# A decoder layer on one core: the groups of work of a pipelined step written in another order on four engines

## What is computed

```
x = x + attn(layernorm(x))      # gated slot attention, 4 heads, 64 slots: a recurrence over time
x = x + xattn(layernorm(x), ctx) # cross attention, 16 heads, 64 keys of ctx, bias from positions, mask
x = x + ffn(layernorm(x))       # mixture of experts: top 2 of 8, capacity 1280, silu(x W1) * (x W3) W2
```

## Time and profile before

| what | value |
| --- | --- |
| median of 3 runs | 1478.4 us (1473.18 to 1479.07) |
| the profiled execution | 1473.74 us, its span 1472.0 us |
| PE matmuls busy | 1366.1 us, 93% of the span |
| PE weight loads busy | 1212.5 us, 82% |
| DVE busy | 949.4 us, 64% |
| ACT busy | 632.6 us, 43% |
| POOL busy | 343.2 us, 23% |
| mean granted TensorE clock | 0.969 of full speed |

### The profile page before, as it was taken

One profiled execution on the slowest core, in us unless ns is written; L12 is line 12 of the kernel. 1 busy time (PEld: TensorE's weight loads), 2 busy tenths in 40 slices (PEclk: granted clock), 3 DMA queues, 4 the chain that ended last, 5 costly groups with the idle time before them and its releaser, 6 DMA issues. The chain is left out here.

```text
span 1472.0 us, 32584 instructions
## 1 busy us (share of the span) xinstructions
PE 1366.1 (93%) x10841; PEld 1212.5 (82%) x10841; DVE 949.4 (64%) x3162; ACT 632.6 (43%) x1596; POOL 343.2 (23%) x524
## 2 busy tenths in 40 slices
PE   7799999999999999999848999999999999999995
PEld 5577777777777777777638999999999999999995
DVE  4578888887877887887654546555564645555442
ACT  2345445544544554544324434443443434444331
POOL 3112222322322322232220222211221112121122
PEclk9799999999999999999858999999999999999998
DMA  2731131101101100110003242321424142241111
GB/s 90 219 99 32 25 109 32 32 17 32 32 17 32 32 21 29 32 32 14 23 29 115 36 120 34 110 36 30 127 31 120 30 115 33 63 94 30 30 23 22
DMA packets 67319, 80.13 MB, mean 54 GB/s; under 512 B 11090, under 2 KB 60723, under 8 KB 67154
## 3 DMA queue, kind: packets, MB, share of 16 engines
q1 hardware_dynamic: 52562, 59.09, 13.1%
q0 software_dynamic: 14592, 18.91, 7.7%
HBM read 44.04 MB, written 33.96 MB: 53 GB/s over the span
## 5 line engine op out<-in xcount | busy, mean ns | idle before, releaser
L856 ACT ACTIVATE h_a<-banks 128x256 f32<-128x256 f32 x320 | 122.4, 383 | 355.0 <-PE banks L1364 351.2
L1298 DVE TENSOR_TENSOR h_f<-banks,h_a 128x256 f32<-128x256 f32 x320 | 135.5, 423 | 154.2 <-ACT h_a L856 149.7
L500 POOL TENSOR_TENSOR idle_g<-half 128x1 f32<-128x1 f32 x144 | 28.8, 200 | 699.2 <-DVE y_s L1317 398.2
L1364 PE MATMUL banks<-xe_t_hi,w_even_hi 128*128 128x256 f32 x640 | 179.4, 280 | 0.0
L1364 PE MATMUL banks<-xe_t_hi,w_odd_hi 128*128 128x256 f32 x640 | 178.6, 279 | 0.0
L1364 PE MATMUL banks<-xe_t_lo,w_even_hi 128*128 128x256 f32 x640 | 177.6, 278 | 0.0
L1364 PE MATMUL banks<-xe_t_hi,w_even_lo 128*128 128x256 f32 x640 | 177.5, 277 | 0.0
L1364 PE MATMUL banks<-xe_t_lo,w_odd_hi 128*128 128x256 f32 x640 | 177.0, 277 | 0.0
L1364 PE MATMUL banks<-xe_t_hi,w_odd_lo 128*128 128x256 f32 x640 | 176.9, 276 | 0.0
L845 ACT ACTIVATE h_t_hi<-h_f 128x256 fp32r<-128x256 f32 x320 | 131.7, 412 | 29.0 <-DVE h_f L1298 29.0
L1305 DVE TENSOR_TENSOR h_t_lo<-h_f,h_t_hi 128x256 fp32r<-128x256 f32 x320 | 133.5, 417 | 6.1 <-ACT h_t_hi L845 4.4
(11 more groups left out here) (240 smaller groups left out, 3505.9 us busy)
## 6 DMA issues: line engine op xcount, KB each, us to landing
raw<-in_w SPq DMA_DIRECT2D x24, 1024.0 KB, 9.3
expert_rows<-empty SPq DMA_DIRECT2D x4, 2580.0 KB, 11.3
xe<-expert_rows SPq DMA_DIRECT2D x40, 258.0 KB, 2.8
xin<-in_x SPq DMA_DIRECT2D x32, 128.0 KB, 2.5
out_dram<-x SPq DMA_DIRECT2D x32, 128.0 KB, 2.0
out_dram<-y_s,token POOLq DMA_INDIRECT x80, 3.8
mask_i<-in_mask SPq DMA_DIRECT2D x32, 32.0 KB, 1.8
expert_rows<-r_xn,send POOLq DMA_INDIRECT x64, 3.0
```

The source lines that it names most:

```text
L500: return pool.tensor_tensor(idle_g[:, i:i + 1], half[:, 0:1], half[:, 0:1], ALU.add)
L856: act.activation(h_a[:, f % 2, :], bank[2 + f % 4][:, 0:GS], ACT.Silu).then_inc(silu_ok, 1)
L1298: dve.tensor_tensor(h_f[:, f % 2, :], bank[2 + f % 4][:, GS:2 * GS], h_a[:, f % 2, :], ALU.mult)\
L1364: last = pe.matmul(dst, lhs, rhs, start=(i == 0), stop=(i == len(pairs) - 1))
```

## The change

The four `step` functions get a new order. PE's step now begins with `counts`, so that the work that closed a step before (all from `sum_gates` to `read_and_positions`) runs on the chunk of the step before: its lags are one greater, and LAGS is 5 instead of 4. A step's boundary is no instruction. What is left when the boundaries are set aside is this:

- PE: `counts` before `o_columns`; `values` before `x_columns`; `r_logits` after `mix` instead of after `f_columns`; `x_scores` after `xo_columns` and `f_columns`, right before `project_vf`, instead of right after `read_out`.
- DVE: `f_statistics` right after `gate_probs`, and `f_norm` ahead of `causal_mix`; `top_two` right after `causal_mix` instead of after `x_less`; `end_states` after the head's squares, `x_maximum` after `head_weights`; `causal_scores` ahead of `x_statistics`; `x_norm` after `slot_logits` and so ahead of `gate_probs`.
- ACT: `x_columns` after `softmax_exp`, `r_columns` after `p_columns`, `router_exp` ahead of `squares`.
- POOL: `send_rows` after `f_power_later` of the next step and so ahead of `head_power`, instead of after `places` at once; `values` after `r_power`. The one-instruction `hold` in it gets a semaphore of its own.

The table of banks follows the new order. No instruction of arithmetic is added or taken away.

```
-LAGS = 4
+LAGS = 5
...
         turns = [
-            [("counts", 4), ("e_cols0", 2), ("read", 0)],
-            [("xo_cols", 3), ("qk", 0), ("scores0", 0), ("mix0", 0)],
-            [("f_cols", 0), ("decay_cols", 0), ("scores1", 0), ("mix1", 0)],
-            [("vf", 0), ("ks_cols", 0), ("logits", 0), ("r_cols", 3)],
-            [("o_cols", 1), ("values", 2), ("sums", 0)],
-            [("x_scores0", 2), ("p_cols", 0)],
-            [("x_scores1", 2), ("gates", 0), ("y", 1), ("e_cols1", 2), ("xq", 1)],
-            [("r_logits", 4), ("xy", 3), ("x_cols", 1)],
+            [("counts", 5), ("e_cols0", 3), ("read", 1)],
+            [("scores0", 1), ("mix0", 1), ("xo_cols", 3), ("qk", 0)],
+            [("decay_cols", 1), ("scores1", 1), ("mix1", 1), ("f_cols", 0)],
+            [("ks_cols", 1), ("logits", 1), ("r_cols", 4), ("vf", 0)],
+            [("o_cols", 2), ("values", 3), ("sums", 1)],
+            [("p_cols", 1), ("x_scores0", 2)],
+            [("gates", 1), ("y", 2), ("e_cols1", 3), ("xq", 2), ("x_scores1", 2)],
+            [("xy", 4), ("x_cols", 2), ("r_logits", 4)],
         ]
...
@@ send_rows
-                hold(0)
+                if later(n, 1):
+                    pool.wait_ge(held_send, n)
+                hold(0).then_inc(held_send, 1)
...
@@ gpsimd
                 run(0, f_power_later)
-                run(2, values)
+                run(5, send_rows)
                 run(1, head_power)
-                run(4, send_rows)
                 run(1, keys)
                 run(3, r_power)
+                run(2, values)
                 run(1, hidden_keys)
                 run(1, x_power)
...
@@ scalar
+                run(1, softmax_exp)
+                run(2, x_columns)
+                run(1, p_columns)
+                run(4, r_columns)
+                run(2, x_queries)
+                run(4, router_exp)
+                run(1, squares)
                 run(0, f_columns)
                 run(3, xo_columns)
                 run(0, f_absolute)
-                run(4, router_exp)
...
                 run(2, e_columns)
-                run(1, x_columns)
-                run(0, softmax_exp)
-                run(3, r_columns)
-                run(0, p_columns)
-                run(1, x_queries)
-                run(0, squares)
...
@@ vector
+                run(1, gate_probs)
                 run(0, f_statistics)
+                run(3, x_denominators)
+                run(1, sum_and_values)
+                run(3, x_outputs)
                 run(0, f_norm_and_context)
-                run(1, end_states)
+                run(1, mix_and_tables)
+                run(4, top_two)
                 run(1, head_squares)
                 run(1, head_squares2)
+                run(1, end_states)
+                run(1, head_weights)
                 run(2, x_maximum)
-                run(1, head_weights)
                 run(1, head_outputs)
                 run(2, x_less)
-                run(4, top_two)
                 run(0, log_gates)
...
                 run(1, residual1)
+                run(0, scores_and_context)
                 run(1, x_statistics)
-                run(0, scores_and_context)
-                run(1, x_norm)
                 run(3, r_norm)
                 run(0, slot_logits)
-                run(0, gate_probs)
-                run(0, sum_and_values)
-                run(2, x_denominators)
-                run(2, x_outputs)
-                run(0, mix_and_tables)
+                run(1, x_norm)
...
@@ tensor (the new order whole)
+                run(5, counts)
+                run(2, o_columns)
+                run(1, sum_gates)
+                run(4, x_project_o)
+                run(1, decay_columns)
+                run(1, ks_columns)
+                run(2, project_o)
+                run(1, scores_and_values)
+                run(3, e_columns)
+                run(1, logits_and_values)
+                run(3, values)
+                run(2, x_columns)
+                run(4, r_columns)
+                run(1, p_columns)
+                run(2, x_queries)
+                run(1, mix)
+                run(4, r_logits)
+                run(1, sum_states)
+                run(1, read_and_positions)
+                run(3, xo_columns)
+                run(0, f_columns)
                 run(2, x_scores)
...
                 run(0, project_vf)
                 run(0, project_qk_and_context)
```

More of the change, by code:

```diff
@@ L285, in decoder_layer @@
         xet_mm, xet_ok, up_mm, silu_ok, gated_ok, dn_mm, y_ok = sems("xet_mm xet_ok up_mm silu_ok gated_ok dn_mm y_ok")
-        about_ok, added, held = sem("about_ok"), sem("added"), sem("held")
+        about_ok, added, held, held_send = sem("about_ok"), sem("added"), sem("held"), sem("held_send")
         x2_stored = [sem(f"x2_stored{i}") for i in range(2)]
@@ L1622, in step @@
             def step(run):
+                run(5, counts)
[19 more added lines that the diff above has]
+                run(0, f_columns)
                 run(2, x_scores)
-                run(0, f_columns)
-                run(4, r_logits)
-                run(3, xo_columns)
                 run(0, project_vf)
                 run(0, project_qk_and_context)
[L1629 to L1646, removed]
             over_chunks(step)
```

## The result

The new kernel takes 1434.4 us (median of 4 runs, 1431.7 to 1437.9); the kernel before took 1477.1 in the same session. The ratio is 0.971, 95% interval 0.968 to 0.974. The forecast was 1437. One of the six executions of the control (experiment 1) took 6559.8 us at a granted clock of 0.191, so the time given there is the median of the other five.

A forecast was written before the change was run, and what follows sets the result against it. PE's list with its waits was taken to set the 21.7 us step. Gains of 27 (steady), 4 (filling) and 9 (emptying) summed to 40 us, giving 1434 for one execution and a median of 1437 us, range 1418 to 1462.

The forecast's parts named there:

- A: PE leg `project_vf` to `decay_columns`, 6.99 us: falls to 6.60, gain 0.39 in three steps of four, nothing in the fourth.
- B and C: PE legs from `decay_columns` to `p_columns`: first one 5.70 to about 5.03 us, gain 0.67; second stays 2.57.
- D: PE leg from `p_columns` to the next `project_vf`: same matmuls in another order, stays 6.68 us.
- The steady part: Third chunk's `project_vf` to the last one's, 29 steps: 0.9 to 1.0 us gained a step, 27 us; bounds 9, 46.
- POOL: `send_rows` (3.11 us) moves between `f_power_later` and `head_power`, ahead of b_rms: about 2 us of cover left.
- Filling: Before the steady part: PE's 4.83 us wait for the second norm goes, bringing 4 us; bounds 0 and 8.
- Emptying: After the last step: waits for `both` (8.1 us) and sends' 3.1 us go; 9 us taken, bounds 3 and 13.
- Experts: Stretch of 692.30 us after the emptying: the change touches nothing of it.
- Rival 2: POOL's slower sends hold the head's power; decides from 3.35 us lateness; step 0.55 slower, +16 us, 1490 us; chance 0.08.
- Rivals 1, 3, 4: 1: same waits renamed, 1456 us, 0.16; 3: silu/recurrence loop, 1475 us, 0.05; 4: PE's loads bound, 1310 us, within 0.03.

The follow-up runs named there:

- experiment 1: The new kernel run again unchanged, as a control: 1430.8 us, ratio 0.969 to the kernel before.
- experiment 8: The new kernel with `one_minus` on ACT behind decay instead of ahead of down: 1437.3 us, ratio 0.974 to the kernel before.
- experiment 5: The new kernel with the first chunk's `mix_and_tables` ahead of the second chunk's `f_norm` again, only at the start: 1442.3 us, ratio 0.976.
- experiment 6, sends_old_place: The new kernel with POOL's order as before, `send_rows` one step earlier, behind `head_power`: 1440.8 us, ratio 0.974.
- Experiment 7: The new kernel with four extra powers (1.05 us each) on POOL behind `send_rows`, ahead of b_rms, in every step: 1486.9 us, ratio 1.008.
- experiment 11: The new kernel with a_s ahead of `residual1` and `r_statistics`, `r_norm` behind `gate_probs`, and PE's `r_columns` behind `p_columns`: 1487.2 us, ratio 1.008.
- scores_late: The new kernel with the masked scores a_s made behind `x_statistics` again: 1461.7 us, ratio 0.990.
- pool_extra4: The new kernel with four extra powers on POOL ahead of b_rms in every step: 1486.9 us, ratio 1.008.
- dve_list_short: The new kernel with a_s ahead of `residual1` and `r_statistics`, `r_norm` behind `gate_probs`, `r_columns` behind `p_columns`: 1487.2 us, ratio 1.008.
- both_lists: `dve_list_short` plus `one_minus` behind decay, `ks_columns` ahead of `x_exp`, and k_s and s_s transposed in two banks: 1489.1 us, ratio 1.009.
- second_norm_late: The new kernel with `f_statistics` and `f_norm` behind `causal_mix` again: 1467.4 us, ratio 0.994.
- top_two_late: The new kernel with `top_two` behind `x_less` again and ACT's `router_exp` back behind `f_absolute`: 1476.3 us, ratio 0.999.

## Why the prediction held, point by point

- **What bounds it**: PE's list with its waits, right as far as it goes. The experiments add what the earlier trace rows can't show: undone alone, three parts cost 25.4, 36.2 and 26.0 us of the steady part, 87.6 together, where all of them had brought 24.1. Each sits in cover that the others opened; the legs' gains add up for the whole, not for one part taken out. Steps of the lower clock are in the 25.4 too, some 8 us of it.
- **The sum**, 42.1 for 40, is closer than its terms, and that is luck: the steady part was 2.9 short and the experts 3.0, filling and emptying were 3.9 and 3.6 over, the last step 0.5. The forecast of 1437 also isn't its own sum: 1434 and the 4.7 us of the median would be 1439.
- **A**, 6.99 to 6.60: as predicted, and ACT is what holds it there (experiment 8).
- **B and C**: 7.56 us for 7.60 predicted; a_s late costs 0.70. **D**: 6.74 for 6.68.
- **The steady part**, 24.1 for 27, within its bounds. The regular step gave 21.94 - 20.90 = 1.04 for 1.06, a sequence's first 0.44 for 0.4. Mis-sized was the product with 29: (3 x 1.06 + 0.4)/4 is 0.895 a step, 26 us, not 27, and the first steps of the trace had little to give (66.61 to 87.44 was 20.83 us already). Of its signs two failed: PE still waits for g_s in the step behind a sequence's first, and no wait for x_xn came.
- **POOL**: 2.4 us of cover for "about 2". Right.
- **Filling**, 7.9 at like clock (the control's 10.8 has less of the lower clock in it) for 4: the term that was too small. I priced the wait and left the projection at 3.78 us; without the wait it ran at the higher clock and took 1.98 (experiment 5 has both back). The Trainium skill, TensorE: Matmul & The Clock Gate, What's actually happening, has the throttled clock as the default that activity lifts. By that rule the prediction named 2 to 4 us more than its 4, and the 7.9 agrees with it.
- **Emptying**, 12.6 for 9: 8 at like clock. The split is borne out only in part: `both`'s waits come back with `top_two`, the sends are worth about 2 us by the estimate in experiment 6, for the 3.1 that I gave them.
- **Experts**, +3.0 for 0: from the first expert transposes on it is 698.6 us for 695.7, and the twelve other profiles, with nothing changed there, have 695.9 to 709.9: no effect.
- **Rival 2** did not come, but its working was wrong: it decides from 3.35 us, I said, and that holds POOL's 2 us of cover, which I had already taken off the 3.9 us of lateness that I set against it. From b_rms on it is 0.35 + 1.0 = 1.35 us. Experiment 7 has 0.27 covered and everything behind it charged in full: at 1.8 us the kernel is already 0.8% slower than before.
- **Rivals 1, 3, 4**: PE has no new waits of a rival's size; the step moved; and PE's loads are busy 467.02 of 604.72 us, 16.1 us a step as before, with no step near that.

## What to carry to other kernels

Read a wait marked "issue" ahead of a matmul against the table of its bank: the product that had the bank before may be evacuated late in another engine's list (experiment 11), and an operand that is early then buys nothing. When an order packs several chains into each other's gaps, don't price one part by taking it out, nor expect the next move to be free. Compare like stretches of two profiles only with the granted clock beside them.

## What the runs showed that was not expected

- In the steady part, where the new kernel's clock is 1.00 throughout, four of the variants show single short stretches at 0.5 again and again: 7 in `scores_late`, 5 in `pool_extra4`, more in `dve_list_short` (with a long one from 164 to 176 us) and `both_lists`. `sends_old_place` and `second_norm_late` have one each, near the start. `top_two_late`, whose PE is busy only 459.88 of 500 us against 478.63 in `scores_late`, shows none. In `scores_late` the fall comes with PE busy 2.90 of the 2.90 us before it. Which order is hit, and by what, stays open.
- The new kernel's emptying, the same program, was granted 0.69 of the clock in one profile and 0.57 in the other, 4.3 us apart.
